# First layer of a four-layer kernel: query parts kept once in DRAM and repeated by the reading transfers, the second step's rows issued behind the landing of the first's

## The reference

```python
a = _layer_norm(audio_kv, ln_gamma, ln_beta)
Q = (hidden_states @ Wq.T).reshape(B, Tt, HEADS, HEAD_DIM).transpose(0, 2, 1, 3)   # B=4, Tt=256, 16 heads of 16
K = (a @ Wk.T).reshape(B, Ta, HEADS, HEAD_DIM).transpose(0, 2, 1, 3)
V = (a @ Wv.T).reshape(B, Ta, HEADS, HEAD_DIM).transpose(0, 2, 1, 3)
scores = jnp.einsum('bhtd,bhsd->bhts', Q, K) * scale
attn = jax.nn.softmax(jnp.where(mask, scores, -inf), axis=-1)
out = jnp.einsum('bhts,bhsd->bhtd', attn, V) ... @ Wo.T
return hidden_states + jnp.tanh(gate) * out
```

## Time and profile before

| | us |
|---|---|
| median of 3 runs | 1354.59 |
| lowest, highest | 1352.16, 1358.65 |
| the profiled execution | 1357.32 |
| its span | 1355.3 |
| PE busy (share of the span) | 1255.6 (93%) |
| DVE, ACT, POOL busy | 808.7, 530.8, 177.6 |
| packets of SP's queue, share of the 16 DMA engines | 28.2% |

### The profile page before, as it was taken

How to read it: one execution, slowest core, us unless ns; L and a number is a source line. 1 busy time by engine, 2 the same in 40 slices (tenths; PEclk the granted TensorE clock), 3 DMA queues, 4 the chain that set the end, 5 groups by cost and what they waited for, 6 DMA issues and landing times.

```text
span 1355.3 us, 18110 instructions
## 1 busy us (share of the span) xinstructions
PE 1255.6 (93%) x6176; PEld 898.4 (66%) x6176; DVE 808.7 (60%) x2374; ACT 530.8 (39%) x1221; POOL 177.6 (13%) x397
## 2 busy tenths in 40 slices
PE   5669989999999868999999699999999999999999
PEld 3347656565657534444443388888888888888877
DVE  4434337585858535678785566666665666666630
ACT  2134353343444323545555334434333434343432
POOL 3122013021212211112010200000000000000000
PEclk8578699999999878999999999999999999999999
DMA  7354502202020344442434551221303030500000
GB/s 249 118 142 137 152 15 111 101 24 101 24 101 24 119 155 127 148 151 98 137 128 141 194 202 34 92 74 52 115 11 125 1 125 1 186 1 1 1 9 24
DMA packets 100379, 127.06 MB, mean 94 GB/s; under 512 B 6720, under 2 KB 78560, under 8 KB 98048
## 3 DMA queue, kind: packets, MB, share of 16 engines
q1 hardware_dynamic: 99664, 125.61, 28.2%
q10 hardware_dynamic: 624, 0.30, 0.1%
HBM read 78.80 MB, written 46.79 MB: 93 GB/s over the span
## 4 chain that ended last, share of the span: by engine, by line
PE 80%; DMA 8%; DVE 2%; ACT 2%; SPq 2%; POOL 2%; issue 2%; ACTq 0%; POOLq 0%; DVEq 0%
PE J L2367 8%; PE TT L2375 8%; PE J L2385 8%; PE S L2341 4%; PE TT L2351 4%; PE OO L2341 4%; PE OO L1053 4%; PE OO L1049 4%; PE J L324 2%; PE J L1053 2%; PE J L1049 2%; PE OO L2585 2%; PE OO L1897 2%; DMA early<-query_parts 2%; PE J L1309 2%; PE S L1049 2%
## 5 line engine op out<-in xcount | busy, mean ns | idle before, releaser
L2443 ACT ACTIVATE PT<-TT 128x512 f32<-128x512 f32 x128 | 76.4, 597 | 283.2 <-PE TT L2351 283.2
L2514 DVE TENSOR_SCALAR QK<-J,cols 128x256 f32<-128x256 f32 x126 | 61.0, 484 | 71.1 <-PE J L2367 71.1
L2478 POOL COPY On<-probs 128x8 f32<-128x8 f32 x128 | 29.1, 227 | 477.1 <-DVE probs L2503 447.8
L2503 DVE TENSOR_SCALAR probs<-probs,inv 128x257 f32<-128x257 f32 x256 | 79.0, 351 | 4.5
L2351 PE MATMUL TT<-ident,probs 128*128 128x128 f32 x512 | 77.4, 274 | 1.7 <-DVE probs L2503 1.7
L2351 PEld LDWEIGHTS TT<-ident,probs 128*128 128x128 f32 x512 | 64.1, 141 | 15.7 <-DVE probs L2503 2.8
L1049 PE MATMUL OO<-weights_a,ctxT 128*128 128x512 f32 x136 | 67.2, 617 | 7.0 <-ACT weights_a L1064 4.0
L2509 DVE COPY km<-TT 128x256 f32<-128x256 f32 x128 | 54.2, 423 | 31.1 <-PE TT L2375 30.8
L1053 PE MATMUL OO<-ctxT,weights_a 128*128 128x512 f32 x136 | 66.4, 610 | 6.4 <-ACT weights_a L1066 3.1
L951 DVE CUSTOM_DVE_ANT_0 mask_b<-S,weights_a 128x256 f32<-128x256 f32 x64 | 24.6, 422 | 70.9 <-PE S L632 70.7
L2495 DVE TENSOR_REDUCE maxes<-S 128x1 f32<-128x257 f32 x128 | 48.4, 420 | 30.8 <-PE S L2341 30.8
(11 more groups left out here) (400 smaller groups left out, 2767.7 us busy)
## 6 DMA issues: line engine op xcount, KB each, us to landing
wide_values<-weights_a SPq DMA_DIRECT2D x64, 256.0 KB, 2.0
wide_keys<-weights_a SPq DMA_DIRECT2D x64, 256.0 KB, 2.1
query_parts<-weights_a SPq DMA_DIRECT2D x48, 192.0 KB, 2.8
weights_a<-wide_keys SPq DMA_DIRECT2D x16, 512.0 KB, 7.0
weights_a<-wide_values SPq DMA_DIRECT2D x16, 512.0 KB, 8.4
early<-wide_keys SPq DMA_DIRECT2D x16, 512.0 KB, 8.0
early<-wide_values SPq DMA_DIRECT2D x16, 512.0 KB, 8.6
weights_a<-key_parts SPq DMA_DIRECT2D x16, 288.0 KB
```

Of the source, the lines that this page charges most:

```text
L2443: act.activation(PT[:, n % 2, :], T0[:, :], ACT.Copy).then_inc(pt3_ready, 1)
L2503: ins = dve.tensor_scalar(P_[n % 2][:, qt, :], P_[n % 2][:, qt, :], inv[:, qt, n % 32:n % 32 + 1], None, ALU.mult)
L2514: dve.tensor_scalar(QK[:, n % 2, 0, 0:S], J0[:, 0:S], head_cols(f"bq{a + 1}")[:, h:h + 1], float(DIM3) ** -0.5, ALU.add, ALU.mult).then_in ...
```

## The change

The diff touches four places, all in the first layer.

- The DRAM tensor of the query parts loses the dimension of the repetitions: 3 x 128 x 256 values for each s.
- `keep_queries0` writes each s once: two transfers for a batch in place of six, each of the same size as before.
- `spread0` reads the query rows of each s with three transfers, one for each part a, of 24 destination rows; the source is 8 rows, repeated by a leading dimension of 3. A step's rows come with eight transfers, two for the keys and six for the queries, in place of four. The bytes are the same.
- `stacked0_sp` waits between `spread0(0)` and `spread0(1)` until all eight transfers of step 0 have landed.

The counts in the waits follow (2 for 6 writes, 8 for 4 reads).

```diff
-        query_parts0 = nc.dram_tensor("query_parts_0", [B, 2, PARTS, PARTS, P, S], BF16).ap()
+        query_parts0 = nc.dram_tensor("query_parts_0", [B, 2, PARTS, P, S], BF16).ap()
...
         def keep_queries0(sp, b):
             sp.wait_ge(queries0_split, b + 1)
             for s in range(2):
-                for c in range(PARTS):
-                    sp.dma_start(query_parts0[b, s, :, c].rearrange("a p n -> p a n"),
-                                 parts0["q"][:, :, s * S:(s + 1) * S]).then_inc(query0_kept, 16)
+                sp.dma_start(query_parts0[b, s].rearrange("a p n -> p a n"),
+                             parts0["q"][:, :, s * S:(s + 1) * S]).then_inc(query0_kept, 16)
...
-            sp.wait_ge(query0_kept, 16 * 2 * PARTS * (b + 1))
+            sp.wait_ge(query0_kept, 16 * 2 * (b + 1))
             for s in range(2):
-                sp.dma_start(q_rows0[m % 4][0:ROWS0, s, :, :],
-                             query_parts0[b, s].rearrange("a c (d h) n -> (a c d) (h n)", d=HALF0)[:, here])\
-                    .then_inc(rows0_landed[m % 4], 16)
+                for a in range(PARTS):
+                    sp.dma_start(q_rows0[m % 4][a * 24:a * 24 + 24, s, :, :],
+                                 query_parts0[b, s, a].rearrange("(d h) n -> d (h n)", d=HALF0)[:, here]
+                                 .unsqueeze(0).to_broadcast([PARTS, HALF0, n_here])).then_inc(rows0_landed[m % 4], 16)
...
             spread0(sp, 0)
+            sp.wait_ge(rows0_landed[0], 16 * 8)
             spread0(sp, 1)
             keep_keys0(sp, 1)
             keep_queries0(sp, 1)
...
-                        pe.wait_ge(rows0_landed[m % 4], 16 * 4 * (m // 4 + 1))
+                        pe.wait_ge(rows0_landed[m % 4], 16 * 8 * (m // 4 + 1))
```

More of the change, by code:

```diff
@@ L599, in stacked0_sp @@
                     sp.wait_ge(key0_kept, 16 * 2 * B)
-                    sp.wait_ge(query0_kept, 16 * 2 * PARTS * B)
+                    sp.wait_ge(query0_kept, 16 * 2 * B)
                     load_values()
@@ L797, in fetch_queries @@
                         act.wait_ge(queries0_split, b)
-                        act.wait_ge(query0_kept, 16 * 2 * PARTS * b)
+                        act.wait_ge(query0_kept, 16 * 2 * b)
                     act.activation(exact0["q"], bank_[:, :], ACT.Copy, scale=DIM0 ** -0.5)
```

## The result

The changed kernel takes 1381.99 us (median of 4 runs, 1379.73 to 1387.75) against 1356.62 us for the kernel before, measured beside it. The ratio is 1.0191, with a 95% interval of 1.0148 to 1.0234, or +25.9 us (+20 to +32). The profiled execution spans 1378.1 us, against 1355.3.

The account below looks back on a forecast made before the run. The prediction held that PE waits in the first layer for row reads, whose key pieces use three of 16 DMA engines. Terms 10.5 + 4.5 + 2 + 5.8 + 0.7 + 3.1 made +26.6 us, median 1381, range 1363 to 1398.

Parts of the forecast that it names:

- step 0: First layer's first rows: writes end 2.7 us sooner, reading 5.8 longer, 1.2 less mixing; +1.9 us, landing at 40.6.
- step 1, with step 0 and the wait: First layer's second rows, issued only after the first land, then read for 16.8 us: landing 58.8 against 48.26, +10.5 us.
- step 2: First layer's third rows: read 5.8 us longer with 1.3 us of cover, leaving +4.5 us (+3 to +4.5).
- clock, up to the issue of step 3: PE's granted clock stays lower for some fills after the wait for step 2: +2 us (0 to +3).
- step 3: First layer's fourth rows, already waited for, so the longer read counts whole: +5.8 us (+3 if mixing loads come behind).
- steps 4 and 5: First layer, rows read back to back: 8.9 us longer after saved writes, against 8.2 us of cover; +0.7 (0 to +3.4).
- step 6: First layer, rows behind batch writes with no cover: 5.8 less 2.7 for fewer writes, +3.1 us (0 to +5.8).
- step 7: First layer's last rows: fill came without a wait, cover not visible in the rows; 0 us (0 to +4).
- The longer read: Each first-layer step's rows: query pieces join the keys on three engines, 15.5 us in place of 9.7, +5.8 a step.
- the fitted overhead: First-layer reads: 1.3 us a step, the 11.0 us of traffic beyond 9.7 us computed for the busiest three engines.
- only the new wait costs: Rival, first layer: longer reads are hidden and only the wait costs, +10.5 us, giving 1365; chance 0.10.
- the first rival: New query pieces keep many engines (12), so reading is no longer and fewer writes gain: -5.4 us, 1349; chance 0.10.

Follow-up runs that it names:

- distinct_no_wait: Changed kernel without its wait, each query piece reading 24 different rows instead of 8 repeated; 1350.17 us against 1356.04 for the kernel before, ratio 0.9964.
- distinct_rows: Changed kernel, wait kept, each query piece reading 24 different rows instead of 8 repeated; 1354.33 us against 1353.9 for the kernel before, ratio 1.0005.
- lead_four: Changed kernel with each query piece's 24 distinct rows taken as 4 x 6, without repetition; ratio 1.0084 to the kernel before.
- lead_two: Changed kernel with each query piece's 24 distinct rows taken as 2 x 12, without repetition; ratio 1.0404 to the kernel before.
- wait_only: Kernel before plus only the wait for step 0's four reads ahead of issuing step 1; 1356.62 us against 1353.9, ratio 1.0018.
- reads_only: Changed kernel without its wait; 1377.93 us against 1353.9 for the kernel before, ratio 1.0189.
- inner_repeat: Changed kernel without its wait, rows reordered so keys repeat inside and queries are read as 8 x 3; 1329.29 us against 1353.9 before, ratio 0.9806.

## Why the prediction was right, point by point

The forecast was 1381 with +26.6 us; the result is 1382.0 with a ratio that makes +25.9. The parts fit less closely than the sum. Each term is compared with the step by which the lateness of the fills grows, from the earlier trace rows to the timeline above; steps 2 and 7 before, which had no wait, filled at 65.79 and 165.77:

```profile
165.77 0.60 PE L632 MATMUL S<-weights_a,early 72*128 72x256 bf16 x4
```

| term | forecast, us | measured, us |
|---|---|---|
| step 0 | +1.9 (not in the sum) | +1.3 |
| step 1, with step 0 and the wait | +10.5 | +9.9 |
| step 2 | +4.5 | +4.4 |
| clock, up to the issue of step 3 | +2 | -0.2 |
| step 3 | +5.8 | +3.3 |
| steps 4 and 5 | +0.7 | +0.8 |
| step 6 | +3.1 | +2.3 |
| step 7 | 0 | +0.3 |
| from step 7's fill to the layer's end | 0 | +3.2 |
| behind the layer | 0 | -1.1 |
| sum | +26.6 | +22.8 (span) |

**What was luck.** That the sum comes within 1 us is luck; that it comes near is not. The forecast puts all 26.6 us ahead of step 7's fill, and the profile has 20.7 there (186.46 less 165.77). The 3.2 us behind it are a fall of the clock that another execution doesn't have (below). A sum of +21 would have lain within the interval of the measured difference, +20 to +32, as well.

The terms are also read against one profile of the kernel before, and that had a slow stretch of its own. Behind a wait of 2.2 us for a maxima copy, the clock of PE was at its lower level nearly all the time from 106.5 to 113.5:

```profile
106.50:113.50 7.00, 7.00 (x44) 4.53 (x43) 2.16 (x9) 2.41 (x4) 1.44 (x7) 0.54 0.45 131
```

From step 3's fill to step 5's that profile takes 38.3 us; distinct_no_wait, with a wait of 1.5 us and the higher level throughout this stretch, takes 34.7. So the +0.8 of steps 4 and 5 would probably be larger against an execution without this fall. How much larger isn't shown, as distinct_no_wait differs in its writes too.

**What bounds the kernel** held. The shares showed three engines for the keys and twelve for the queries; distinct_rows, lead_four and lead_two confirm that a piece's engines follow its leading dimension. The Trainium skill ("DMA: Bandwidth & Descriptors", section "Why a DMA increments its semaphore by 16 and not by 1") gives the largest number up to 16 that divides the slowest dimension of both sides. The runs agree for 12, 8, 4, 3 and 2: shares of 0.75, 0.51, 0.26, 0.19 and 0.13.

**The longer read**, +5.8 us a step, was right where a step's rows move alone. At step 2 the read took 18.1 us from issue to fill, and it was forecast as 18.2. The cover of 1.3 us was read rightly too: 5.7 less 1.3 is the +4.4 by which the lateness grows at step 2.

One price inside this sum was wrong, and the fitted overhead made up for it. The prediction gave each of the twelve engines of the query pieces 25.3 GB/s, the rate of the keys, which the half microsecond at 28.00 with 303 GB/s seemed to bear out. The three next half microseconds moved only 164, 180 and 246. At step 2 before, from 54.5 to 58.0, while the query pieces ran, the rate was 180 GB/s, so they took some 3.5 us and not 1.9. With the 7.8 us of the keys that already makes up the 11.0 of the trace, and no overhead is left. On three engines the rate did hold: the changed kernel's step 2 moved its bytes from 64.0 to 79.5 at 76 GB/s, and the other 2.6 us of its read lie ahead of the traffic (2.0) and behind it (0.5).

**The wait** was priced right in sum only. The prediction put the whole +10.5 under the step behind the wait. The runs split it: 7.1 us come from the longer reads without any wait, and 2.7 from the wait. The rival "only the new wait costs" had +10.5 as the price of the wait, and so was priced wrongly as well as unlikely; wait_only gives +2.4 (0 to +5).

**The writes** were mis-sized at their place. I let step 0 gain 2.7 us by four fewer writes and 1.2 by the missing mix. Measured alone, the first gives 0.9 (37.82 in distinct_no_wait against 38.74) and the second 0.5 (38.26 in wait_only); together they give 2.2 (36.56 in distinct_rows). In the whole kernel the writes are worth 4.9 us, near the first rival's 5.4. That rival's time of 1349 agrees with the 1350.2 of the kernel that has its condition and no wait; with the change's wait it comes out as no change.

**The clock** was right in kind and wrong in place. After step 2's fill PE did run at the lower level, for 5.6 us where it had been 3.7 before. But the next issue on SP came 9.7 us behind that fill, where it had come 10.0 behind it before, so nothing of this reached step 3. The clock cost 3.1 us where I had put nothing, behind step 7's fill. From 188.0 to 194.5 the granted clock is 0.50 (third row of the windows above), and the work from L680 to L687 takes 6.9 us where it took 3.8 before. In the kernel before, the clock stayed at the higher level over the same work, and 7.0 us held 66 matmuls where 6.5 us held 40:

```profile
167.00:174.00 7.00, 7.00 (x66) 5.61 (x64) 4.57 (x24) 3.75 (x7) 0.46 (x3) 1.00 0.01 3
```

PE had waited 0.7 us at 181.4 and 1.6 us at 186.5. In reads_only it had waited 1.3 and 1.5 us at the same places, and the layer ended without that loss: it took 30.1 us from step 7's fill to the last turning of outputs (183.30 to 213.41), the same as in the kernel before (165.77 to 195.89). So the loss belongs to the execution, and a wait of that size alone doesn't fix it. Why the clock fell in one and not in the other stays open. The timed runs show the same variation: the four of reads_only took 1371.75 and 1373.52 us at mean granted clocks of 0.949 and 0.948, and 1382.33 and 1382.49 at 0.944.

**Step 3** is the term that failed in size: 5.8 forecast, 3.3 measured. PE's wait for it grew from 10.2 to 12.3 us and not to the 16 that the prediction named as a sign. I had named the cause as its low end (loads that mix in before and come behind after), and in the two runs with the loads moved it makes up 1.1 of the 2.5 us.

## What to carry to other kernels

A transfer that builds repeated rows should not have the repetition as its leading dimension: look at the DMA share in a window where only it moves, and a share of 0.19 with a rate near 76 GB/s means that 13 of 16 engines stand idle. Order the rows so that a dimension of 8 or 12 leads and the repetition lies inside. Here that was worth 25 us together with the single write, and some 20 without it (an estimate: 24.6 less the 4.9 of distinct_no_wait). A saved write (4.9 us) or a wait in the queue (some 2.4 us) was worth far less here than the engines that the reads lost (26 us), so count the engines before and after for each transfer that an edit rewrites.

## What the runs showed of the hardware that I had not expected

- SP's issue of a transfer costs more with three dimensions than with two: six pieces of 24 plain rows took 2.53 us (0.42 each), as 4 x 6 rows 3.92 (0.65), as 8 x 3 rows 4.15 (0.69), and as 3 x 8 repeated rows 4.30 (0.72). I had counted 0.5 for each.
- SP's issue slows when reads on few engines are still under way. In reads_only, where step 1 is issued straight behind step 0, its six query pieces took 10.34 us to issue instead of 4.30. In inner_repeat, at the same place but with reads on 12 and 8 engines, they took 4.14.

```profile
23.42 4.30 SPq L556 DMA_DIRECT2D km<-query_parts  x6
...
30.82 10.34 SPq L556 DMA_DIRECT2D km<-query_parts  x6
```

- The small copy of the first maxima, issued by ACT while step 2's rows were read, took 7.0 us in the changed kernel (61.97 to 68.95) against the 7.6 of the earlier trace rows. The longer read did not make this copy slower.
